# First self attention of a Perceiver block: query, key and value projections in split float32r products, one stacked low-rank product

## What is computed

```python
def _L0_attn_ref(x, Wq, bq, Bq, Aq, Wk, bk, Bk, Ak, Wv, bv, Bv, Av, Wo, bo, Bo, Ao):
    def lora_linear(x, W, b, Bm, Am):
        out = jnp.einsum('bld,od->blo', x, W) + b
        upd = jnp.einsum('blr,or->blo', jnp.einsum('bld,rd->blr', x, Bm), Am)
        return out + SCALING * upd          # RANK = 16, SCALING = 0.5
    q = _split(lora_linear(x, Wq, bq, Bq, Aq))     # 16 heads of 32
    k = _split(lora_linear(x, Wk, bk, Bk, Ak))
    v = _split(lora_linear(x, Wv, bv, Bv, Av))
    attn = jax.nn.softmax(jnp.einsum('bhqd,bhkd->bhqk', q, k) * SCALE, axis=-1)
    out = jnp.einsum('bhqk,bhkd->bhqd', attn, v)
    return lora_linear(out, Wo, bo, Bo, Ao)
```

## Time and profile before

| what | value |
|---|---|
| median of 3 runs (lowest, highest) | 1515.16 us (1513.21, 1516.91) |
| the profiled execution, its own time | 1516.96 us |
| its span | 1515.1 us |
| mean granted clock of PE, share of full speed | 0.957 |
| projection block, first matmul to first matmul of the attention core | 446.50 to 486.24 us |

### The profile page before, as it was taken

The page is one execution under the profiler, slowest core; times in us unless marked ns, Lnnn a source line. Parts: engine busy times, 40 slices in busy tenths (PEclk is TensorE's granted clock), DMA queues, the critical chain, the costliest instruction groups (busy, mean ns, idle before and its releaser), DMA issues. The chain is left out here.

```text
span 1515.1 us, 31884 instructions
## 1 busy us (share of the span) xinstructions
PE 1415.0 (93%) x11772; PEld 1087.6 (72%) x11772; DVE 999.5 (66%) x1651; ACT 783.7 (52%) x1130; POOL 78.4 (5%) x71
## 2 busy tenths in 40 slices
PE   6999999999979989999989999969999688899998
PEld 4677776777735479999977877846666365799997
DVE  6666677666645467666538777768999333676664
ACT  3677777777741545554422222327887103555552
POOL 0000000000010300000011121110000100000000
PEclk9999999999989979999999999978999769899999
DMA  5333443333223077656115233237785120676662
GB/s 167 73 89 86 121 104 85 83 83 89 49 76 141 1 244 264 206 197 209 37 47 168 106 126 109 84 87 164 170 175 116 49 53 9 207 254 211 213 216 75
DMA packets 133457, 190.94 MB, mean 126 GB/s; under 512 B 74972, under 2 KB 96702, under 8 KB 130175
## 3 DMA queue, kind: packets, MB, share of 16 engines
q1 hardware_dynamic: 133391, 190.04, 43.6%
HBM read 153.86 MB, written 17.48 MB: 113 GB/s over the span
## 5 line engine op out<-in xcount | busy, mean ns | idle before, releaser
L187 PE MATMUL psum<-m_x_hi,m_gu_hi 128*128 128x256 f32 x780 | 222.8, 286 | 3.2 <-DVE m_h L2381 2.9
L188 PE MATMUL psum<-m_x_hi,m_gu_lo 128*128 128x256 f32 x780 | 222.1, 285 | 0.0
L189 PE MATMUL psum<-m_x_lo,m_gu_hi 128*128 128x256 f32 x780 | 222.0, 285 | 0.0
L1527 DVE TENSOR_REDUCE x_peaks<-psum 128x2048 f32 (+1 forms) x64 | 146.4, 2291 | 51.6 <-PE psum L1419 51.6
L187 PE MATMUL psum<-x_w_hi,x_ctx_hi 128*128 128x256 f32 x512 | 159.0, 311 | 0.0
L187 PEld LDWEIGHTS psum<-m_x_hi,m_gu_hi 128*128 128x128 f32 x780 | 150.7, 193 | 6.9 <-DVE m_h L2381 3.3
L188 PEld LDWEIGHTS psum<-m_x_hi,m_gu_lo 128*128 128x128 f32 x780 | 150.7, 193 | 1.5
L189 PEld LDWEIGHTS psum<-m_x_lo,m_gu_hi 128*128 128x128 f32 x780 | 150.5, 193 | 0.0
L188 PE MATMUL psum<-x_w_hi,x_ctx_lo 128*128 128x256 f32 x512 | 145.1, 283 | 0.0
L189 PE MATMUL psum<-x_w_lo,x_ctx_hi 128*128 128x256 f32 x512 | 144.9, 283 | 0.0
L1657 DVE TENSOR_TENSOR e_wqp<-e_wqp,x_probs 128x1024 f32<-128x1024 f32 x124 | 141.7, 1220 | 3.1 <-ACT x_probs L1672 2.8
(11 more groups left out here) (310 smaller groups left out, 2777.9 us busy)
## 6 DMA issues: line engine op xcount, KB each, us to landing
m_gu_raw<-in_m_gu SPq DMA_DIRECT2D x41, 768.0 KB, 4.3
e_w<-x_keys_dram SPq DMA_DIRECT2D x45, 512.0 KB, 6.9
m_gu_raw<-in_m_gu SPq DMA_DIRECT2D x18, 1024.0 KB, 5.0
x_ctx_raw<-in_ctxT SPq DMA_DIRECT2D x64, 256.0 KB, 2.7
m_dn_raw<-in_m_down SPq DMA_DIRECT2D x16, 768.0 KB, 4.3
m_dn_raw<-in_m_down SPq DMA_DIRECT2D x18, 512.0 KB, 5.1
x_keys_dram<-x_keys_hi SPq DMA_DIRECT2D x16, 512.0 KB, 3.2
x_keys_dram<-e_wqp SPq DMA_DIRECT2D x16, 512.0 KB, 2.6
```

The lines of the kernel that those rows point to most:

```text
L187: pe.matmul(out, a[0], b[0], start=start, stop=False, skip_group_check=True)
L188: pe.matmul(out, a[1], b[0], start=False, stop=False, skip_group_check=True)
L189: return pe.matmul(out, a[0], b[1], start=False, stop=stop, skip_group_check=True)
L1527: dve.tensor_reduce(peaks[:, t, 4 * m:4 * m + 4, bass.ds(k, 1)].rearrange("p h k -> p (h k)"), g.psum[:, at:at + BANKS, :], AX, ALU.max).t ...
```

## The change

- The three low-rank products become one: `down` holds each 16-row matrix with a copy of itself, 32 columns wide, so that q, k and v stand side by side at partitions 0, 32 and 64 of one result [96, 256]. `low` and `up` are stacked the same way; `up` becomes [96, 512]. The output projection's `up` is a tensor of its own, `up_o` (17 rows), loaded at the end.
- ACT rounds `xnT` and the weights of k, q and v to float32r in chunks of 128 features; DVE subtracts. There are two buffers for the split weights, so the value weights are split only after the keys are done.
- PE makes the three projections with `product3`, and the 17-row update and bias as a float32 matmul as before. It waits for the split of each chunk in the first m (or t). The keys no longer wait for `low` before they begin, but only before their first 17-row matmul. Values go to banks 2 and 3.
- The work ahead on `kv_raw` moves: ACT rounds the four pieces, between taking `qT` and taking `v`, and POOL subtracts.
- The output weights go into the buffer of the key weights, so their load waits for the keys' split.

```diff
-        w = [sb("w" + n, [P, NC, D], F32) for n in names]
-        down = sb("down", [P, NC, 4, RANK], F32)
-        up = sb("up", [RANK + 1, 4, D], F32)
-        low = sb("low", [RANK + 1, 4, L], F32)
+        w = [sb("w" + n, [P, NC, D], F32) for n in names[:3]]
+        w.append(w[1])
+        down = sb("down", [P, NC, 4, 2 * RANK], F32)
+        up = sb("up", [3 * 32, D], F32)
+        up_o = sb("up_o", [RANK + 1, D], F32)
+        low = sb("low", [3 * 32, L], F32)
...
                     for c in range(NC):
-                        last = pe.matmul(g.bank[n][0:RANK, 0:L], down[:, c, n, :], g.xnT[:, c, :],
-                                         start=(c == 0), stop=(c == NC - 1))
-                last.then_inc(low_made, 1)
-                pe.wait_ge(up_loaded, 16)
-                pe.wait_ge(lowo_made, 3)
-                for n in (1, 0):
-                    pe.wait_ge(w_loaded[n], 16)
-                    for m in range(NC):
-                        o = g.bank[4 + 2 * n + m // 2][:, (m % 2) * L:(m % 2 + 1) * L]
...
+                        sp.dma_start(kv_raw[:, c, :], A["x1_wkvT"][:, c, :]).then_inc(kv_loaded[c], 16)
+                    sp.wait_ge(w_split, NC)
+                    load_weight(sp, 3)
+                    sp.dma_start(up_o[:, :], A["a0_up_o"]).then_inc(up_o_loaded, 16)
+
+                @block.gpsimd
+                def _(pool):
+                    pool.memset(low[:, :], 1.0).then_inc(low_cleared, 1)
+                    pool.memset(k_pad[:, :, :], 0.0).then_inc(pad_cleared, 1)
+                    for c in range(NC):
+                        pool.wait_ge(kv_rounded, c + 1)
+                        pool.tensor_tensor(g.x1_w_lo[:, c, :], kv_raw[:, c, :], g.x1_w_hi[:, c, :].bitcast(F32),
+                                           ALU.subtract)
...
+                    pe.wait_ge(down_loaded, 16)
+                    for c in range(NC):
+                        last = pe.matmul(g.bank[0][0:3 * 32, 0:L], down[:, c, 0:3, :].rearrange("p n r -> p (n r)"),
+                                         g.xnT[:, c, :], start=(c == 0), stop=(c == NC - 1))
+                    last.then_inc(low_made, 1)
+                    pe.wait_ge(up_loaded, 16)
+                    pe.wait_ge(x_split, 1)
+                    for i, n in enumerate(ORDER[:2]):
+                        for m in range(NC):
+                            o = g.bank[4 + 2 * n + m // 2][:, (m % 2) * L:(m % 2 + 1) * L]
+                            for c in range(NC):
+                                if m == 0:
+                                    pe.wait_ge(w_split, NC * i + c + 1)
+                                product3(pe, o, halves(i, (c, slice(m * P, (m + 1) * P))),
+                                         [b[:, c, :] for b in (x_hi, x_lo)], c == 0, False)
+                            if i == 0 and m == 0:
+                                pe.wait_ge(lowo_made, 3)
+                            last = pe.matmul(o, up[low_rows(n), m * P:(m + 1) * P], low[low_rows(n), :], start=False,
+                                             stop=True, skip_group_check=True)
+                        last.then_inc((q_done, k_done)[n], 1)
...
+                    dve.wait_ge(x_rounded, 1)
+                    dve.tensor_tensor(x_lo[:, :, :], g.xnT[:, :, :], x_hi[:, :, :].bitcast(F32),
+                                      ALU.subtract).then_inc(x_split, 1)
+                    dve.wait_ge(low_cleared, 1)
+                    dve.wait_ge(low_made, 1)
...
+                    split_w(0)
+                    split_w(1)
+                    dve.wait_ge(k_done, 1)
+                    split_w(2)
...
+                    act.activation(x_hi[:, :, :], g.xnT[:, :, :], ACT.Copy).then_inc(x_rounded, 1)
+                    round_w(0)
+                    round_w(1)
+                    act.wait_ge(k_done, 1)
+                    round_w(2)
+                    act.wait_ge(q_done, 1)
+                    for b in range(2):
+                        act.activation(qT[:, 2 * b:2 * b + 2, :].rearrange("p c n -> p (c n)"), g.bank[4 + b][:, :],
+                                       ACT.Copy)
                     for c in range(NC):
-                        pe.matmul(g.bank[t][:, :], g.xnT[:, c, t * P:(t + 1) * P], w[2][:, c, :],
...
+                        act.wait_ge(kv_loaded[c], 16)
+                        act.activation(g.x1_w_hi[:, c, :], kv_raw[:, c, :], ACT.Copy).then_inc(kv_rounded, 1)
+                    act.wait_ge(v_done, 1)
+                    for t in range(NT):
+                        act.activation(v[:, t, :], g.bank[2 + t][:, :], ACT.Copy)
```

More of the change, by code:

```diff
@@ L847, in stage_attn0, with low_rows @@
         kv_loaded, kv_rounded = [sem(f"kv_loaded{c}") for c in range(NC)], sem("kv_rounded")
+        x_rounded, x_split, w_rounded, w_split, up_o_loaded = (
+            sem(n) for n in ("x_rounded", "x_split", "w_rounded", "w_split", "up_o_loaded"))
+        def low_rows(n):
+            return slice(32 * n, 32 * n + RANK + 1)
         def load_weight(sp, n):
@@ L858, in stage_attn0 @@
         stage_layernorm(nc, g, "ln_a0_", prefetch)
[L859 to L880, removed]
-                    for c in range(NC):
-                        last = pe.matmul(g.bank[n][0:RANK, 0:L], down[:, c, n, :], g.xnT[:, c, :],
-                                         start=(c == 0), stop=(c == NC - 1))
-                last.then_inc(low_made, 1)
-                pe.wait_ge(up_loaded, 16)
-                pe.wait_ge(lowo_made, 3)
-                for n in (1, 0):
-                    pe.wait_ge(w_loaded[n], 16)
-                    for m in range(NC):
-                        o = g.bank[4 + 2 * n + m // 2][:, (m % 2) * L:(m % 2 + 1) * L]
-                        for c in range(NC):
[L892 to L896, removed]
-                    for c in range(NC):
-                        pe.matmul(g.bank[t][:, :], g.xnT[:, c, t * P:(t + 1) * P], w[2][:, c, :],
[L899 to L923, removed]
-                for c in range(NC):
-                    dve.wait_ge(kv_loaded[c], 16)
-                    dve.tensor_copy(g.x1_w_hi[:, c, :], kv_raw[:, c, :]).then_inc(kv_rounded, 1)
-                    dve.wait_ge(kv_rounded, c + 1)
-                    dve.tensor_tensor(g.x1_w_lo[:, c, :], kv_raw[:, c, :], g.x1_w_hi[:, c, :].bitcast(F32),
-                                      ALU.subtract)
-            @block.scalar
-            def _(act):
-                act.wait_ge(q_done, 1)
-                for b in range(2):
-                    act.activation(qT[:, 2 * b:2 * b + 2, :].rearrange("p c n -> p (c n)"), g.bank[4 + b][:, :],
-                                   ACT.Copy)
-                act.wait_ge(v_done, 1)
-                for t in range(NT):
-                    act.activation(v[:, t, :], g.bank[t][:, :], ACT.Copy)
@@ L957, in _ @@
                 for c in range(NC):
-                    last = pe.matmul(g.bank[0][0:RANK, 0:L], down[:, c, 3, :], outT[:, c, :],
+                    last = pe.matmul(g.bank[0][0:RANK, 0:L], down[:, c, 3, 0:RANK], outT[:, c, :],
                                      start=(c == 0), stop=(c == NC - 1))
@@ L965, in _ @@
                                   start=(c == 0), stop=False)
+                    pe.wait_ge(up_o_loaded, 16)
                     pe.wait_ge(low2_made, 1)
-                    pe.matmul(g.bank[2 + t][:, :], low[:, 3, t * P:(t + 1) * P], up[:, 3, :],
+                    pe.matmul(g.bank[2 + t][:, :], low[low_rows(0), t * P:(t + 1) * P], up_o[:, :],
                               start=False, stop=True).then_inc(out_done, 1)
@@ L972, in _ @@
                 dve.wait_ge(low2, 1)
-                dve.tensor_scalar(low[0:RANK, 3, :], g.bank[0][0:RANK, 0:L], LORA, None,
+                dve.tensor_scalar(low[0:RANK, :], g.bank[0][0:RANK, 0:L], LORA, None,
                                   ALU.mult).then_inc(low2_made, 1)
@@ L2509, in lay_out @@
                                              for w in (wk, wv)], axis=0).T)
-    out["a0_down"] = np.ascontiguousarray(np.stack([chunked(a[f"L0_attn_B{n}"].T) for n in "qkvo"], axis=2))
-    out["a0_up"] = np.ascontiguousarray(np.stack(
-        [np.concatenate([a[f"L0_attn_A{n}"].T, a[f"L0_attn_b{n}"][None]], axis=0) for n in "qkvo"], axis=1))
+    out["a0_down"] = np.ascontiguousarray(np.stack([chunked(np.repeat(a[f"L0_attn_B{n}"], 2, axis=0).reshape(
+        RANK, 2, D).transpose(1, 0, 2).reshape(2 * RANK, D).T) for n in "qkvo"], axis=2))
+    up = [np.concatenate([a[f"L0_attn_A{n}"].T, a[f"L0_attn_b{n}"][None]], axis=0) for n in "qkvo"]
+    out["a0_up"] = np.ascontiguousarray(np.concatenate([np.concatenate([u, u])[:32] for u in up[:3]], axis=0))
+    out["a0_up_o"] = np.ascontiguousarray(up[3])
     for n in "qkvo":
```

56 lines of the change are left out of this document (55 added, 1 removed).

## The result

| | kernel before | changed kernel |
|---|---|---|
| median of 16 runs each (lowest, highest), us | 1515.03 (1512.49, 1518.82) | 1519.78 (1516.04, 1524.18) |
| ratio, 95% interval | | 1.0029 [1.0018, 1.0040] |
| the profiled execution, us | 1516.96 | 1518.11 |
| its span, us | 1515.1 | 1516.3 |

The interval says 2.7 to 6.1 us slower; the forecast was 1515.9, with a range up to 1518.8. I measure the change by the length of its stage in the profile: from the first to the next of POOL's `norm_rstd` rows, the layer norm that opens each stage. That stage went from 90.03 us (441.85 to 531.88) to 93.25 (443.71 to 536.96), **+3.22 us**. The stages beside it hold no changed line and differ between single executions by a few us either way (the second cross attention took 437.28 and 433.64), so I compare stages, and medians with their intervals, not single spans.

What follows compares the result with a forecast made beforehand. PE and the two hand-overs around it bound the projection block; -3.3 us for the earlier core start plus 2.0 and 2.0 for clock losses gave +0.7, so 1515.9 us, range 1511.6 to 1518.8.

Steps and rivals of the forecast that it cites:

- The clock, twice: PE pauses before the keys and before the attention core each lose full clock, costing 2.0 us each.
- Start of the keys: Low-rank product of 8 instructions ends at 450.1, 3.6 us gained; key weights' splits run from 452.0 to 453.8.
- Pace of the products: Projections: 2.28 us per key or query chunk against 2.54; values 8.4 us in all against 9.47.
- POOL holds the end: End of projection block: POOL's four subtractions of 2.39 us end at 482.6, core starts at 482.9 against 486.24, -3.3 us.
- The second loss of the clock: PE idle 3.7 us after the values, so the attention core starts at half speed and loses 2.0 us.
- The clock holds: Rival: only the first PE pause survived, -1.3, 1513.9; both, -3.3, 1511.9 us; chance 0.20.
- POOL doesn't hold the end: Rival: POOL's subtraction is quicker or overlaps more before the core, no second clock loss, -3.5, 1511.7 us; chance 0.12.
- The slower rival: Key weights land as late as before because `up` was not what held them: +4.8, 1520.0 us; chance 0.10.

Runs made afterwards that it cites:

- the grouping: The four 17-row matmuls of the keys, and those of the queries, placed behind all 48 products; alone in the changed kernel, with the right start flag, 1516.90 us.
- e2: Changed kernel with the four kv_raw subtractions moved from POOL back to DVE, behind its context splits: 1515.25 us.
- e5: Changed kernel with keys' and queries' 17-row matmuls behind all 48 products, but a wrong start flag that left out products: 1514.28 us.
- e8: Changed kernel without the stacked low-rank product (three separate 16-row products, up in 17 rows): 1523.39 us.
- e4: Kernel before with the stacked low-rank product only, other products still float32: 1512.46 us.
- e6: Changed kernel with filler matmuls, subtractions on DVE and 17-row matmuls behind the products, wrong start flag leaving out products: 1507.89 us.
- e9: Changed kernel with filler matmuls, subtractions on DVE and 17-row matmuls behind the 48 products, right start flag: 1508.26 us.
- e3: Changed kernel with filler matmuls on zeros ahead of the keys and the kv_raw subtractions on DVE: 1511.22 us.
- e7: Kernel before with the stacked low-rank product and 17-row matmuls behind the products, all float32, some products left out: 1510.03 us.
- e10: Changed kernel with keys' and queries' 17-row matmuls behind their 48 products and the start flag set by bank, nothing else: 1516.90 us.

## Why the prediction was wrong, step by step

Counted from the first low-rank matmul, so that the later start of the stage drops out:

| step | forecast | measured | difference |
|---|---|---|---|
| key weights' last split done | 7.3 | 7.7 | +0.4 |
| keys done, with the clock's loss | 17.2 | 19.95 | +2.75 |
| queries done | 26.3 | 28.95 | +2.65 |
| POOL done, from there on | 11.8 | 12.5 | +0.7 |
| core starts | 38.4 | 41.75 | +3.35 |
| the core's own loss of clock | 2.0 | 1.2 | -0.8 |
| sum against the kernel before | +0.7 | +3.2 | +2.5 |

(The core's loss: from its start to the low-rank product behind it 34.55 us, before 33.36.)

- **The step that failed** is *The clock, twice*: "I take it as lost, and got back after some 4 us of dense work at half speed, of which half, 2.0 us, is lost time". Lost it was, but it came back only after 10.2 us of busy PE. The loss was 4.4 us: 1.1 in the first m, 1.75 and 1.5 in the second and third (4.00 and 3.76 against 2.25). The upper end of its bound, 2.1, was wrong too: the two returns that it came from, at 541.70 and at 446.50, had no 17-row matmuls between the others. With the grouping, which makes the keys like the first of them, 3.4 us came out twice. The trace of the kernel before held a warning that the prediction didn't read; its rows stand below the list. This term alone, +2.4, moves the forecast from "no change" to the 3 us that a measurement tells as slower.
- **Start of the keys**: right. Low-rank product of 8 instructions in 3.70 us, weights landed by 452.0, 3.7 us behind its start (before: 8.3; forecast: 2.5, which cost nothing since DVE was not ready), roundings and split of `xnT` hidden. Mis-sized by 0.4: the scalings took 1.31 where I carried over 1.07, and began 0.2 later.
- **Pace of the products**: right, 2.25 a chunk against 2.28. The values took 8.1 us against 8.4, which nobody waited for.
- **POOL holds the end**: right as a mechanism, and e2 shows it: without it the core starts 3.6 us earlier. Three subtractions took 2.33 to 2.35 us, the one beside DVE's split of a context chunk (479.39 to 480.61) took 3.43. The bound of 1.2 for this stood in the range, but 2.39 for all four was taken; 1.08 was the price.
- **The second loss of the clock**: right in kind, 1.2 instead of 2.0, because the clock held for most of the pause and fell only 0.5 us ahead of the core.
- **The rivals.** "The clock holds" and "POOL doesn't hold the end" both fell. The slower rival named late weights; those came early. The result was slower by another mechanism, one that the forecast had in its sum and priced too low.

The 3.2 us of the two profiled executions lie within the 2.7 to 6.1 of the medians' interval. Where in the other executions the rest of the median's 4.75 lies, if it is more than scatter, was not measured.

The warning stands in the second layer's self attention of the kernel before, a stage that the change doesn't touch. Groups of 16-row matmuls alternate there with 128-row ones, PE has no break from 1220.06 us on, and yet the clock falls at 1221.8 and is back only at 1242.3, 3.3 us after PE has gone over to 128-row matmuls alone (timeline of PE, then a window):

```profile
1226.31 1.67 PE L1079 MATMUL psum<-a_k_pad,a_q_pad 16*128 16x256 f32 x16
1227.91 1.03 PE L1084 MATMUL psum<-a_mask,a_ident_bf 128*128 128x256 bf16 x4
...
1238.98 3.53 PE L1148 MATMUL psum<-a_wv,x_norm_T 128*128 128x128 f32 x16
```

```profile
1226.00:1238.00 12.00, 12.00 (x98) 7.83 (x96) 8.63 (x10) 0.00 (x0) 0.00 (x0) 0.50 0.01 5
```

Eleven of the twelve kernels' profiles show the same 20.5 us at half speed in this stage; in e5 the clock stayed at full speed over these groups, so they don't make it fall in every execution.

What stays open: why matmuls with few rows delay the clock's return. That they do is shown by one edit in five profiles and agrees with this stage. No run varied the number or the rows of the 17-row matmuls, so their few rows can't be told from the short breaks in the stream of products where the shape changes, nor is it shown why e8 had the clock back 3.4 us sooner than the changed kernel and e2 with the same matmuls.

## What to carry to other kernels

When a faster product opens a pause on PE, price the pause and the return to full clock from rows with the same mix of matmuls as follows there, not from any return in the trace; filling the pause with matmuls on zeros gave 3.8 us here. Put matmuls with few rows together behind the full ones, with the start flag once per PSUM bank. Before moving work to an idle engine, ask whether it then ends last ahead of a barrier: twice the duration on POOL was a 3.4 us longer pause on PE.

## What the runs showed of the hardware that I had not expected

- In the keys half speed lasted 6.8 to 10.2 us with PE busy throughout when a 17-row matmul followed every 12 products, 3.4 us without. Under a busy PE with groups of 16-row matmuls it lasted 20.5 us.
- The same 1.42 us pause kept the clock in five executions (before, e2, e4, e6, e9) and lost it, 0.3 to 0.5 us after PE had started again, in two (e3, e7).
- POOL's two-input subtraction and DVE hold each other up in both directions. In e10, where POOL ran from 472.20 on, DVE's rounding of a context chunk took 2.88 us and its split 3.28, against 0.69 and 1.23 in e9, where POOL was idle (e10, timeline of DVE):

```profile
471.42 1.23 DVE L963 TENSOR_TENSOR e_ctx_lo<-a_ctx_raw,e_ctx_hi 128x1024 fp32r<-128x1024 f32 x1
472.56 2.88 DVE L961 CAST e_ctx_hi<-a_ctx_raw 128x1024 fp32r<-128x1024 f32 x1
475.48 3.28 DVE L963 TENSOR_TENSOR e_ctx_lo<-a_ctx_raw,e_ctx_hi 128x1024 fp32r<-128x1024 f32 x1
```

  The Trainium skill, "GPSIMD Engine Reference", section "Key points", says that GpSimd shares its SBUF interfaces with VectorE and contends with DVE instructions that have two SBUF inputs or run in a 2-port perf mode. The split's row agrees for two inputs; the cast has one input and is hit as well, and no row shows in which mode it ran.
